# Summing edges into windows: each 80- or 96-column weight matrix as three products of at most 32 columns

## The reference

```python
h = jnp.maximum(_layernorm(x, axis=-1), 0.0)
# _L0_gnn_ref:
h = feat @ W_node.T
rf = review_feat @ W_review.T            # 64 features per edge
m = (h[src_idx] + rf) * edge_w
rst = jax.ops.segment_sum(m, dst_idx, num_segments=N_NODES)
x = x + rst
```

## Time and profile before

| | |
|---|---|
| median of 3 runs | 1766.9 us (1765.85 to 1771.57) |
| the profiled execution | 1771.62 us |
| its span, first to last instruction | 1769.5 us |
| busy of PE, DVE, POOL, ACT | 1544.8, 1455.6, 1247.3, 970.8 us |
| mean granted clock of TensorE | 0.942 of full speed |

### The profile page before, as it was taken

The page is one execution under the profiler, slowest core; times in us unless marked ns, Lnnn a source line. Parts: engine busy times, 40 slices in busy tenths (PEclk is TensorE's granted clock), DMA queues, the critical chain, the costliest instruction groups (busy, mean ns, idle before and its releaser), DMA issues.

```text
span 1769.5 us, 75737 instructions
## 1 busy us (share of the span) xinstructions
PE 1544.8 (87%) x25040; PEld 1524.7 (86%) x25040; DVE 1455.6 (82%) x3393; ACT 970.8 (55%) x4245; POOL 1247.3 (70%) x1177
## 2 busy tenths in 40 slices
PE   0119998999989899999989998998989998999977
PEld 0019998999989899999989898998989898999975
DVE  7998887888888787888888787878878887878864
ACT  1114364665656564756656564756656564756653
POOL 2287777777777777777777777777777777777400
PEclk9659999999999999999999999999999999999965
DMA  3524345454545445454444454454545454554443
GB/s 116 92 36 113 100 114 114 110 122 103 125 106 128 112 114 127 104 129 109 118 113 111 116 120 116 118 125 105 118 110 114 115 125 109 122 130 100 119 86 48
DMA packets 513913, 195.34 MB, mean 110 GB/s; under 512 B 475071, under 2 KB 496196, under 8 KB 513212
## 3 DMA queue, kind: packets, MB, share of 16 engines
q1 hardware_dynamic: 474853, 178.88, 39.9%
q0 software_dynamic: 36000, 9.29, 5.9%
q10 hardware_dynamic: 2609, 1.55, 0.5%
HBM read 186.67 MB, written 2.92 MB: 107 GB/s over the span
## 4 chain that ended last, share of the span: by engine, by line
PE 46%; DVE 24%; issue 12%; DVEq 8%; POOL 6%; ACT 2%; DMA 1%; ACTq 0%; POOLq 0%; SPq 0%
PE found L1110 26%; PE seg L1143 11%; POOL vals_p L530 6%; DVE big L770 5%; PE seg L1134 5%; DVEq L875 4%; PE edge_h L1124 3%; DVE masked L824 3%; DVEq L867 2%; DVE perm L860 2%; DVE masked L838 1%; DVE mid L845 1%; ACT mid L592 1%; DVE by_rank L715 1%; DVE by_rank L714 1%
## 5 line engine op out<-in xcount | busy, mean ns | idle before, releaser
L530 POOL DMA_INDIRECT vals_p<-h_ext,idx_t x1125 | 1228.7, 1092 | 350.9 <-issue 330.6
L1110 PE MATMUL found<-table,big 128*128 128x112 f16 (+2 forms) x16384 | 870.6, 215 | 57.8 <-DVE by_rank L888 32.3
L1110 PEld LDWEIGHTS found<-table,big 128*128 128x128 f16 x16384 | 846.1, 100 | 63.9 <-DVE by_rank L888 34.9
L592 ACT ACTIVATE sel_p<-hit_p,wgt_t 128x64 f32<-128x64 f16 x1125 | 292.8, 335 | 429.2 <-DVE hit_p L845 416.2
L592 ACT ACTIVATE mid<-mid,wgt_t 128x64 f32<-128x64 f16 x2000 | 500.1, 333 | 36.8 <-DVE mid L845 34.9
L1143 PE MATMUL seg<-mid 128*96 128x64 f32 x4000 | 400.4, 256 | 15.9 <-ACT mid L612 11.3
L1143 PEld LDWEIGHTS seg<-mid 128*96 128x96 f32 x4000 | 379.3, 173 | 18.0 <-ACT mid L592 11.8
L770 DVE TENSOR_SCALAR big<-low_all,own 128x2004 f16<-128x2004 f16 x516 | 361.2, 742 | 2.8 <-DMA low_all<-low_dram 2.8
L879 DVE SCALAR_TENSOR_TENSOR acc<-seg,count_s,acc 96x64 f32 x400 | 112.2, 280 | 168.5 <-issue 126.8
L1134 PE MATMUL seg<-sel_p,vals_p 128*80 128x64 f32 x2250 | 201.8, 237 | 6.9 <-DMA vals_p<-h_ext,idx_t 6.9
L1134 PEld LDWEIGHTS seg<-sel_p,vals_p 128*80 128x80 f32 x2250 | 183.3, 154 | 7.8 <-DMA vals_p<-h_ext,idx_t 3.8
(11 more groups left out here) (131 smaller groups left out, 546.1 us busy)
## 6 DMA issues: line engine op xcount, KB each, us to landing
low_all<-low_dram SPq DMA_DIRECT2D x128, 501.0 KB
mid<-in_edge_attr_dram SPq DMA_DIRECT2D x400, 160.0 KB
vals_p<-in_edge_attr_dram SPq DMA_DIRECT2D x232, 160.0 KB
vals_p<-h_ext,idx_t POOLq DMA_INDIRECT x1125
big<-in_dst_dram SPq DMA_DIRECT2D x1, 1562.5 KB
big<-in_edge_weight_dram SPq DMA_DIRECT2D x1, 1562.5 KB
h_ext<-mid SPq DMA_DIRECT2D x2, 781.2 KB
low_all<-low_dram ACTq DMA_DIRECT2D x2, 501.0 KB
```

What stands on the lines that cost most here:

```text
L530: pool.indirect_dma_start(vals_p[:, q % RP, j, R:F], None, h_ext, bass.IndirectOffsetOnAxis(ap=idx_t[:, q * J + j:q * J + j + 1], axis=0), ...
L592: last = nc.scalar.activation(sel[:, j, :], hit[:, j, :], ACT.Copy, scale=wgt_t[:, bass.ds(tile + j, 1)])
L1110: last = nc.tensor.matmul(found[x % 2][:, r * P:r * P + n], hot[:, x // 2 % 2, a, col:col + P], rows, start=(a == 0 and part == 0), stop=( ...
```

## The change

The columns of the weight matrix of each tile are cut at 32 and 64. Each part is a product of its own, with the same moving matrix, and writes its own 32 (or last 16) partitions of the same PSUM window. So a tile of kind p takes products of 32, 32 and 16 columns, a tile of kind s three of 32. Neither the sums nor their order over tiles change, and semaphores are as before: the last product of the group signals.

```diff
+                parts_p = ((0, 32), (32, 64), (64, 80))
+                parts_s = ((0, 32), (32, 64), (64, 96))
 
                 def sum_p(q, turn_of_slot, x):
...
                     for j in range(J):
-                        last = nc.tensor.matmul(seg_p(x), vals_p[:, slot, j, :], sel_p[:, slot_of(x), j, :],
-                                                start=(j == 0), stop=(j == J - 1))
+                        for low, high in parts_p:
+                            last = nc.tensor.matmul(seg_p(x)[low:high, :], vals_p[:, slot, j, low:high], sel_p[:, slot_of(x), j, :],
+                                                    start=(j == 0), stop=(j == J - 1))
                     last.then_inc(summed_p, 1)
 
                 def sum_s(u, g):
...
                     for j in range(J):
-                        last = nc.tensor.matmul(seg_s(g), vals_s[:, g % RS, j, :], sel_s[:, g % RS, j, :],
-                                                start=(j == 0), stop=(j == J - 1))
+                        for low, high in parts_s:
+                            last = nc.tensor.matmul(seg_s(g)[low:high, :], vals_s[:, g % RS, j, low:high], sel_s[:, g % RS, j, :],
+                                                    start=(j == 0), stop=(j == J - 1))
                     last.then_inc(summed_s, 1)
```

## The result

The changed kernel took 1760.78 us (median of 6 runs, 1758.43 to 1764.58), the kernel before on the same chip 1770.22 (6 runs): a ratio of 0.9953, 95% interval 0.9936 to 0.9971. It is faster by 9.4 us or 0.5%, where 20 us were forecast. The profiled span is 1762.5 us after 1769.5.

The account below looks back on a forecast made before the run. TensorE was taken to bound most of the loop, POOL and DVE close behind. Its terms, -133 + 108 (loop), -2 + 7 (first list), nothing (last stage), made 20 us less: 1766.9 - 20 = 1747 us, range 1722 to 1835.

Parts of the forecast that it names:

- The parts run side by side: In TensorE's sums: a set of three parts costs what one costs, 58 ns, saving 133 us in 15 lists.
- Rivals three and four: In the sums: loads in series, 1936 to 2067 us, chance 0.07; everything in series, about 2370 us, chance 0.05.
- The price of a switch: Whole array to columns and back, twice per block of sums: 0.24 us each, 108 + 7 us more.
- POOL's busy time unchanged: Sign expected in the changed kernel's profile: the gathers keep POOL busy as long as before.
- the 30 us that POOL leaves: Main loop: however fast TensorE gets, POOL's gathers let it end only about 30 us earlier.
- rival one: Switches nearly free, POOL sets the end: 42 us less, 1725 us; low end of the likeliest case, chance 0.60.
- I let them count in full: Main loop: TensorE's 20 us less, well under POOL's 30, pass wholly into the kernel's time.
- The last stage: 25 groups s at half clock: 12 us less against 12 us of switches, nothing in sum.
- rival two: TensorE's instruction fetches come late, 0.3 us per block of sums: 1819 us; chance 0.17, shared with dearer switches.
- The clock: Sign against the forecast: TensorE's clock falls mid-run, each us at half clock costing up to half a us.

Follow-up runs that it names:

- p alone: The kernel before with only the sums of kind p cut in three parts, kind s whole: 1802.34 us, ratio 1.0183.
- s alone: The kernel before with only the sums of kind s cut in three parts, kind p whole: 1762.8 us, ratio 0.996.

## Why the prediction was right in sign and wrong in size

- **The parts run side by side: right.** 58 ns a pass was forecast, 56 measured in the median. The mean over whole blocks is 58.8 ns for s and 59.8 for p, because some passes run at the half clock and the first pass of a block behind `unsort` takes 80. In the 15 lists that is (85.4 - 58.8) x 3750 + (73.4 - 59.8) x 2100 ns = 128 us, where the forecast had 133. Rivals three and four are out.
- **The price of a switch: mis-sized.** "I take the full 0.24", twice in a block, made 108 + 7 us. The rows show 0.11 in and 0.066 out: 40 us in 225 blocks. TensorE's loop thus saved some 90 us, and not 25. The nearest row was a length of a record whose end is modelled, and the next load doesn't wait for all of it.
- **The step that failed: "POOL's busy time unchanged", and with it the 30 us that POOL leaves.** By my own sum, cheap switches meant rival one, 1725 us, with POOL setting the end. POOL did set it: the lag behind the last gather fell from 25.2 to 3.7 us, its real waits are 6.4 us in 14 places less 0.3 each, some 2 us. But the sum took POOL's end as fixed, and the 30 us were reckoned from the gathers of before, and they grew by 24 ns each, 27 us in 1125. So the last gather came 21 us later and took nearly all of it back. The rows shown give the median of 947; the mean of 1092 said that something was already holding some of them, and the question what would happen to these when the order in time changes wasn't asked.
- **"I let them count in full": wrong.** TensorE's saving in the loop counts for nothing (98.7 us a list in both); what was gained lies behind the last gather.
- **The last stage: mis-sized, and the sign hangs on it.** Nothing was forecast, 6.6 us came (with the tail), 14 us of the stage at a clock that the kernel before didn't get. The spans differ by 7.0 us. So that the kernel got faster at all comes nearly whole from a term that the sum put at nothing: the right sign is in good part luck. That 1761 lies in the range is luck too: a switch priced twice too high and gathers that grew offset each other.
- **Instruction supply, rival two: seen, but not in its place.** Not inside the sums but at the start of a list, 3.81 us for 1.45. In the changed kernel it costs nothing measurable; it costs p alone 15 us.
- **The clock:** from 206 to 1686 us it stood at 1.2 GHz for 137 us and not 55, after stretches in which TensorE waits. From 206 to 1600 us the look-ups took 775 us for 767. Since POOL sets the pace, I count no time for it.
- **Open:** why the gathers meet a permutation 159 times and not 134. The same count comes with s alone (153), not with p alone (130), so it goes with POOL being the bound; no run set the two engines' order on its own. 6 of the 27 us are also left unexplained.

## What to carry to other kernels

When an engine with 87% is relieved, ask of the next one not only how much it idles but whether its operations keep their length: a mean well above the median (1092 against 947 ns) says that another engine is stretching some of them, and their number can change with the timing. Cut a narrow weight matrix into parts of 32 columns and keep them in long blocks, since each change of width costs about 0.1 us. By the medians of this kernel it pays from some 14 passes a block on where a pass saves 16 ns, and from eight on where it saves 29 (estimates from the steps above). Undo the halves of a change one by one: the half for p was worth less than nothing when alone, and nearly all of the gain came with s alone.

## What the runs showed of the hardware

- Three float32 products with at most 32 weight columns each and 64 moving columns: 56 ns, against 85 for one of 96 and 73 for one of 80. In parts of 64 and 32, the two together: 244 ns.
- A change between products of the whole width and parts of 32: 0.11 us more in, 0.07 out, and up to 0.05 in the step behind it.
- An indirect transfer on GpSimd of 0.94 us took 1.47 beside one permutation of 0.48 us on VectorE that reads two tensors, 1.88 beside two of them, and 1.07 beside five one-tensor operations of 0.95 us together.
- Where a loop's start falls in the stream of instructions decided whether TensorE ran 8, 52 or all 64 look-ups of a list before it stood still, for 0 to 3.8 us; 23 idle instructions ahead of it gave p_only 15 us.
